# Squares of the queries in the second attention: two heads, two parts, one pass

## The chip, the cores and the metric

The kernel runs on one core of a Trainium2 chip. The metric is device time in microseconds (us), the median of several runs. The inputs are fixed, all in 32-bit floats; everything from the first layer norm to the last output is one program.

## The reference, cut to what matters

The program computes two layers on 625 nodes with 768 features: graph convolutions, attention with random features, and feed-forward parts, the last of them a mixture of experts. The change lies in the attention of the second layer:

```python
def _phi(t, random_features):                  # t: 12 heads, 625 nodes, 64
    norm_sq = 0.5 * jnp.sum(t * t, axis=-1, keepdims=True)
    proj = jnp.einsum('bhnd,md->bhnm', t, random_features)      # 256 features
    return jnp.exp(proj - norm_sq) * (1.0 / math.sqrt(M))
q_p = _phi(q, random_features)
k_p = _phi(k, random_features)
kv = jnp.einsum('bhnm,bhnd->bhmd', k_p, v)
out = jnp.einsum('bhnm,bhmd->bhnd', q_p, kv)
normalizer = jnp.einsum('bhnm,bhm->bhn', q_p, jnp.sum(k_p, axis=2))[..., None]
out = out / (normalizer + 1e-06)
```

For each query and head, minus half of the sum of its 64 squares is added to each of its 256 projections, ahead of the exponential.

## The kernel before, in words

`phase_attend` (L259) is called twice, the second time with `second=True`; only that call is touched. It treats the 12 heads as 6 pairs. A pair's queries lie with the feature on the partitions: head 0 in rows 0 to 63, head 1 in rows 64 to 127 (`own(hd)`; `other(hd)` is the other 64 rows), and 628 columns of nodes, in two halves of 314.

A 32-bit product is made of parts. A value is split into a high part, rounded by a copy into the type F32R (ScalarE), and a low part, the rest (a subtraction on VectorE, or on GpSimd for the squares). `qk[:, QUERIES, hd]` holds one head's high part in its own 64 rows and its low part in the other 64, so that one pass over 128 rows adds both.

The squares are laid out in another way before the change: `sqf` (in `x_sb`) holds the full squares of both heads, `sq[:, a, 0, :]` their high part and `sq[:, a, 1, :]` their low part, each with both heads in its 128 rows (`a` is 1 for keys, 0 for queries). ScalarE writes `sqf` and the high part with two activations of 128x628 (`squares`, L607 and L608) and GpSimd the low part (`square_low`, L354).

TensorE makes the query features in `features_q` (L434): for each of four tiles `m` of 128 features (two for head 0, two for head 1), four matmuls against the random features (L454), then four with `nh` as the weights (L462): parts `a` = 0, 1 times column halves `h` = 0, 1. `nh` is 128x512 with -0.5 in one head's rows and 0 in the other's, so that it picks the head. `key_norms` (L400) uses two of its columns (L409).

The order of the work is written out by hand, each engine with a queue of its own, tied by semaphores. For pair `p`:

- TensorE: `key_norms`, five tiles of key features (L428), with the projections of pair `p+1` between them (L191); four tiles of query features with projections between them; keys times values (L514, 40 matmuls); three more projections; `attend` (L191, out of `m_phiq`, `m_kv`). `attend` waits for `kv_lo`, which VectorE signals at L859.
- ScalarE: five key tiles, each two exponentials (L647) and a copy (L651); the high parts of the keys of `p+1` (L595); for each query tile an exponential (L669) and one that writes the high part (L670), with the key squares of `p+1` after tile 0; a weight chunk's high part (L128); the parts of kv (L684, L688); the query high parts of `p+1`; the denominators (L711); and `squares(p+1, QUERIES)`, which stands right ahead of the key tiles of `p+1`.
- VectorE: the low parts of the five key tiles (L815), with two quarters of a reciprocal (L773) after tiles 0 and 2; key low parts (L764); query low parts (L835) with two more reciprocals and a product (L777) ahead of tile 2; the weight chunk's low part (L139); kv (L853 to L859); copies (L885).
- GpSimd: the low parts of the squares, keys and queries in turn.

ScalarE's exponential of key tile `t` (from tile 2 on) waits for the low part of tile `t-2` (`pk_lo`), which frees its buffer `pf`. TensorE's query tile `m` (from 2 on) waits for the high part of tile `m-2` (`pq_hi`).

Ahead of the pairs, the last five value tiles (`values(2)`, L365) run on TensorE, with the squares of pair 0, a chunk's split (L128, L139) and the value splits (L583, L740) on the other engines; a value tile waits for the low part of the last but one.

Of the kernel before, what the change touches and what calls it, by code (L numbers as in the profile page):

```python
# [6 lines left out]
F32 = mybir.dt.float32  # L7
F32R = mybir.dt.float32r
# [9 lines left out]
P = 128  # L18
# [177 lines left out]
def halves(t):  # L196

    return t.rearrange("p (h n) -> p h n", h=2)
# [60 lines left out]
def phase_attend(k, name, second, rf=None):  # L259
# [3 lines left out]
    with ExitStack() as ctx:  # L263
# [17 lines left out]
        if second:  # L281
            scratch = k.x[:].rearrange("p t d -> p (t d)")
            pf = scratch[:, 0:2 * NT].rearrange("p (a n) -> p a n", a=2)
            sqf = scratch[:, 2 * NT:4 * NT].rearrange("p (a n) -> p a n", a=2)
            den = scratch[:, 4 * NT:5 * NT]
            sq = k.sb(f"{name}_sq", [P, 2, 2, NT], F32R)
            nh = k.sb(f"{name}_nh", [P, 512], F32R)
            key_norm = k.sb(f"{name}_key_norm", [P, 2 * TT], F32)
            tiny = k.sb(f"{name}_tiny", [P, 1], F32)
            k.x_dram = k.nc.dram_tensor("x_dram", (NODES, D), F32).ap()  # L290
        else:
            bv, bq, bp = k.v_bias, k.qk_bias, k.out_bias
        s = signals(k, name, (
            "saved", "rf_in", "chain", "ones_set", "rf_turned", "rf_bd", "rf_hi", "rf_ready", "kn_mm", "kn_f", "v_mm", "v_f", "v_hi",
            "v_lo", "qk_mm", "qk_hi", "qk_lo", "sq_hi", "sq_lo", "pk_mm", "pk_f", "pk_hi", "pk_lo",
            "pq_mm", "pq_f", "pq_hi", "pq_lo", "by_mm", "by_act", "by_dve", "kv_mm", "kv_part", "kv_f", "kv_hi", "kv_lo", "at_mm", "den_f", "num_f",
            "at_out"))
        st.freed.update({n: (s["v_mm"], TT * (c + 1)) for c, n in enumerate(V_CHUNK)})
# [7 lines left out]
        def qk_count(p, a):  # L306
            return 2 * p + (1 if a == KEYS else 2)
# [34 lines left out]
        @block.gpsimd  # L342
        def _(pool):
            k.clear_last(pool)

            def square_low(p):
                for a in (KEYS, QUERIES):
                    pool.wait_ge(s["sq_hi"], qk_count(p, a))
                    if p >= 1:
                        if a == KEYS:  # L350
                            pool.wait_ge(s["pk_mm"], TT * p)
                        else:
                            pool.wait_ge(s["pq_mm"], 4 * p)
                    pool.tensor_tensor(sq[:, a, 1, :], sqf[:, a, :], sq[:, a, 0, :].bitcast(F32), ALU.subtract)\  # L354
                        .then_inc(s["sq_lo"], 1)

            if second:
                for p in range(PAIRS):
                    square_low(p)

        @block.tensor
        def _(pe):
# [37 lines left out]
            def key_norms(p):  # L400
                pe.wait_ge(s["sq_lo"], qk_count(p, KEYS))
                if p >= 1:
                    pe.wait_ge(s["pk_f"], TT * p)
                    pe.wait_ge(s["pq_hi"], 4 * p)
                    pe.wait_ge(s["den_f"], 2 * p - 1)
                    pe.wait_ge(s["num_f"], 2 * p - 1)
                for t in range(TT):
                    for a in range(2):
                        mm = pe.matmul(norm_bank()[0:TS[t], 2 * t:2 * t + 2], sq[:, KEYS, a, t * P:t * P + TS[t]],  # L409
                                       nh[:, MF - 1:MF + 1], start=(a == 0), stop=(a == 1))  # L410
                mm.then_inc(s["kn_mm"], 1)

            def features_k(p):
# [20 lines left out]
            def features_q(p):  # L434
                for m in range(4):
                    i = p * 4 + m
                    if m == 0:
                        pe.wait_ge(s["qk_lo"], qk_count(p, QUERIES))
                        if p == 0:
                            pe.wait_ge(s["v_lo"], 3 * TT)  # L440
                        elif second:
                            pe.wait_ge(s["den_f"], 2 * p)
                            pe.wait_ge(s["num_f"], 2 * p)
                        else:
                            pe.wait_ge(s["num_f"], 2 * p)
                    if m == 1:
                        pe.wait_ge(s["pk_hi"] if second else s["pk_lo"], TT * (p + 1))
                    if m >= 2:
                        pe.wait_ge(s["pq_hi"] if second else s["pq_lo"], i - 1)
                    pair = query_pair(m)  # L450
                    hd, e = divmod(m, 2)
                    for a in range(2):
                        for h in range(2):
                            mm = pe.matmul(pair[:, h, 0:HN], rf2[:, a, e * P:(e + 1) * P],  # L454
                                           qk[:, QUERIES, hd, h * HN:(h + 1) * HN],
                                           start=(a == 0), stop=(a == 1 and not second))
                    if second:
                        if m == 0:
                            pe.wait_ge(s["sq_lo"], qk_count(p, QUERIES))
                        for a in range(2):  # L460
                            for h in range(2):
                                mm = pe.matmul(pair[:, h, 0:HN], nh[:, m * P:(m + 1) * P],  # L462
                                               sq[:, QUERIES, a, h * HN:(h + 1) * HN], start=False, stop=(a == 1))
                    mm.then_inc(s["pq_mm"], 1)
                    if second and p == PAIRS - 1 and m == 1:
                        lead_unit(0)
                    if second and m < 3:
                        project_unit(p + 1, KD + m)
                    elif m == 1:
                        for u in range(KD, KD + 3):  # L470
                            project_unit(p + 1, u)
# [98 lines left out]
        def _(act):  # L570
# [29 lines left out]
            def squares(p, a):  # L600
                src = qk_pair[a][:, :, 0:HN]
                if p == 0:
                    act.wait_ge(s["saved"], 16 * len(ROWS))
                else:
                    act.wait_ge(s["sq_lo"], qk_count(p - 1, a))
                act.wait_ge(s["qk_lo"], qk_count(p, a))
                act.activation(halves(sqf[:, a, :]), src, ACT.Square)  # L607
                act.activation(halves(sq[:, a, 0, :]), src, ACT.Square).then_inc(s["sq_hi"], 1)  # L608

            if not second:  # L610
                ring_high(act, st, 1)
# [110 lines left out]
        def _(dve):  # L722
            link = Link(dve, s["chain"])
            if second:
                dve.memset(vt[:, :, :, DH + 1:DH + 2].bitcast(F32), 0.0)
                dve.memset(kvf[:], 0.0)
                dve.memset(tiny[:], 1e-6)
                dve.memset(nh[:].bitcast(F32), 0.0)
                link(dve.memset(vt[:, :, :, DH:DH + 1].bitcast(F32), 1.0))
                for hd in range(2):  # L730
                    ins = dve.memset(nh[own(hd), hd * MF:(hd + 1) * MF].bitcast(F32), -0.5)
                link(ins)

            def v_low(i):
# [3514 lines left out]
```

## Time and profile before

| what | us |
|---|---|
| median of 3 runs | 1971.12 |
| lowest and highest run | 1968.50, 1972.91 |
| span of the profiled execution, first to last instruction | 1967.0 |
| TensorE busy in it | 1883.6 (96%) |
| VectorE busy | 1205.9 (61%) |
| ScalarE busy | 872.9 (44%) |
| GpSimd busy | 93.9 (5%) |

Of the profiled execution the profile gives the span alone; the runs' median is 4.1 us above it. The second attention's pairs lie between about 992 and 1157 us of the span. In the rows, PE is TensorE, PEld its weight loads, ACT is ScalarE, DVE is VectorE, POOL is GpSimd; a row's text in brackets is the idle time of the engine before it and what ended it.

### The profile page before, as it was taken

The page shows a single profiled execution, that of the slowest core. Times are in us where ns is not written, and L with a number is a line of the kernel's source. Part 1 is how long each engine was busy: PE and PEld are TensorE (multiplying, and loading weights), DVE is VectorE, ACT ScalarE, POOL GpSimd, SP SyncE. Part 2 cuts the span into 40 slices and gives each one's busy share as a digit, 9 for nine tenths or more (in the row PEclk, how much of TensorE's full clock was granted, in tenths as well). Part 3 has the DMA queues.
Part 4 walks back from the last instruction along what each step waited for, and adds up shares of the span by engine and source line. Part 5 has one row for each costly group of instructions (what it writes and reads, how often), then busy time and mean ns, then how long its engine had stood idle before and what let it go on. Part 6 is the DMA issues. An engine that isn't in the chain of part 4 may idle for free. (4 is left out here: it accounts for less than half of the span.)

```text
span 1967.0 us, 32303 instructions
## 1 busy us (share of the span) xinstructions
PE 1883.6 (96%) x13051; PEld 1776.8 (90%) x13051; DVE 1205.9 (61%) x1909; ACT 872.9 (44%) x1176; POOL 93.9 (5%) x84
## 2 busy tenths in 40 slices
PE   5899899999999999998999989899999999999999
PEld 4899789999999999998899989798878888888899
DVE  8467786444343345445557777675666668889732
ACT  6456622222111212214377762423655557777620
POOL 0000000000000000000011000100111101100000
PEclk7899999999999999999999999899999999999999
DMA  3311235121111112110211041424877679999831
GB/s 92 98 41 41 61 105 124 57 57 57 58 57 57 52 45 85 49 49 17 90 33 33 17 142 52 160 77 165 296 234 245 211 231 332 369 379 375 296 119 40
DMA packets 157962, 250.53 MB, mean 127 GB/s; under 512 B 11949, under 2 KB 86189, under 8 KB 157460
## 3 DMA queue, kind: packets, MB, share of 16 engines
q1 hardware_dynamic: 152532, 231.21, 35.3%
q0 software_dynamic: 5040, 17.56, 3.7%
q8 instruction: 89, 1.46, 0.3%
q14 instruction: 29, 0.24, 0.0%
q10 hardware_dynamic: 272, 0.07, 0.0%
HBM read 228.80 MB, written 20.01 MB: 126 GB/s over the span
## 5 line engine op out<-in xcount | busy, mean ns | idle before, releaser
L183 PE MATMUL psum<-products_room 128*128 128x512 f32 (+2 forms) x2160 | 457.2, 366 | 3.1 <-DVE re_credit L3728 2.0
L183 PEld LDWEIGHTS psum<-products_room 128*128 128x128 f32 (+1 forms) x2160 | 388.5, 187 | 47.1 <-issue 2.3
L183 PE MATMUL psum<-ring_hi,xt_sb 128*128 128x256 f32 (+3 forms) x1920 | 357.0, 284 | 9.7 <-PEq L1285 2.8
L3625 DVE TENSOR_TENSOR products_room<-moe_raw,products_room 128x1536 fp32r<-128x1536 f32 x179 | 312.4, 1754 | 76.8 <-ACT products_room L3524 76.4
L3524 ACT ACTIVATE products_room<-moe_raw 128x1536 fp32r<-128x1536 f32 x179 | 266.0, 1489 | 151.9 <-PE psum L183 83.6
L183 PEld LDWEIGHTS psum<-ring_hi,xt_sb 128*128 128x128 f32 (+1 forms) x1920 | 301.2, 189 | 11.5 <-issue 6.3
L183 PE MATMUL psum<-ring_lo,xt_sb 128*128 128x256 f32 (+3 forms) x960 | 271.4, 283 | 0.0
L183 PEld LDWEIGHTS psum<-ring_lo,xt_sb 128*128 128x128 f32 (+1 forms) x960 | 181.5, 189 | 0.0
L183 PE MATMUL psum<-ring_hi,gnn_sb 128*128 128x256 f32 (+1 forms) x810 | 150.0, 286 | 5.4 <-DVE gnn_sb L1188 3.6
L139 DVE TENSOR_TENSOR ring_lo<-ring_raw,ring_hi 128x1536 fp32r<-128x1536 f32 (+1 forms) x64 | 119.4, 1865 | 50.6 <-ACT ring_hi L128 50.5
L191 PE MATMUL psum<-xt_sb,ring_hi 128*128 128x314 f32 x744 | 140.0, 310 | 0.3
L128 ACT ACTIVATE ring_hi<-ring_raw 128x1536 fp32r<-128x1536 f32 (+1 forms) x65 | 101.9, 1568 | 81.5 <-PE psum L191 32.2
L183 PEld LDWEIGHTS psum<-ring_hi,gnn_sb 128*128 128x128 f32 (+1 forms) x810 | 127.2, 191 | 6.3 <-issue 4.3
L191 PE MATMUL psum<-xt_sb,products_room 128*128 128x314 f32 x864 | 127.3, 309 | 2.1 <-DVE products_room L4068 1.1
L191 PEld LDWEIGHTS psum<-xt_sb,products_room 128*128 128x128 f32 x864 | 126.0, 189 | 2.8 <-issue 1.4
L1702 ACT ACTIVATE g_y<-psum 128x256 fp32r<-128x256 f32 (+3 forms) x100 | 37.7, 378 | 198.6 <-PE psum L1635 104.0
L1751 DVE TENSOR_TENSOR g_y<-psum,g_y 128x256 fp32r<-128x256 f32 (+3 forms) x100 | 41.5, 417 | 134.2 <-ACT g_y L1702 134.0
L1656 PE MATMUL psum<-gnn_sb,g_y 128*128 128x314 f32 (+1 forms) x780 | 117.2, 308 | 0.0
L183 PE MATMUL psum<-ring_lo,gnn_sb 128*128 128x256 f32 (+1 forms) x405 | 115.7, 286 | 0.0
L191 PEld LDWEIGHTS psum<-xt_sb,ring_hi 128*128 128x128 f32 x744 | 114.5, 189 | 1.0 <-issue 1.0
L1656 PEld LDWEIGHTS psum<-gnn_sb,g_y 128*128 128x128 f32 (+1 forms) x780 | 114.3, 190 | 0.3 <-DVE g_cnt L1727 0.3
L191 PE MATMUL psum<-xt_sb,ring_lo 128*128 128x314 f32 x372 | 84.7, 309 | 0.0
(532 smaller groups left out, 2756.8 us busy)
## 6 DMA issues: line engine op xcount, KB each, us to landing
moe_raw<-in_L_ffn_Wg_r SPq DMA_DIRECT2D x60, 768.0 KB, 6.1
moe_raw<-in_L_ffn_Wu_r SPq DMA_DIRECT2D x60, 768.0 KB, 6.0
moe_raw<-in_L_ffn_Wd_r SPq DMA_DIRECT2D x60, 768.0 KB, 8.7
ring_raw<-in_L_gnn_w_rel SPq DMA_DIRECT2D x18, 896.0 KB, 5.1
ring_raw<-in_L_mix_W_qkv SPq DMA_DIRECT2D x24, 384.0 KB, 4.3
ring_raw<-in_L_gnn_w_rel SPq DMA_DIRECT2D x9, 768.0 KB, 4.5
ring_raw<-in_L_gnn_w_root SPq DMA_DIRECT2D x6, 896.0 KB, 5.1
count_total_dram<-gnn_sb POOLq DMA_DIRECT2D x3, 1570.0 KB, 11.2
```

What stands on the lines that cost most here:

```text
L128: act.activation(ring.hi[:, g % RING_SLOTS, 0:size], ring.raw[:, g % RING_SLOTS, 0:size], ACT.Copy).then_inc(ring.hi_done, 1)
L139: dve.tensor_tensor(lo, raw, hi.bitcast(F32), ALU.subtract).then_inc(ring.lo_done, 1)
L183: mm = pe.matmul(out, lhs[a], rhs[b], start=(first and i == 0), stop=(last and i == 2))
L191: mm = pe.matmul(bank_pair[:, h, 0:HN], lhs[a], rhs(b, h), start=(first and i == 0), stop=(last and i == 2))
L1656: mm = pe.matmul(pair[:, h, 0:HN], y[0:TS[t], v % 2, t, a, col + m * P:col + (m + 1) * P], k.C[0:TS[t], r, t, h * HN:(h + 1) * HN], start= ...
L1702: act.activation(y[0:TS[t], v % 2, t, 0, 0:w], k.banks[i % 3][0:TS[t], 0:w], ACT.Copy).then_inc(s["y_hi"], 1)
L1751: dve.tensor_tensor(y[0:TS[t], v % 2, t, 1, 0:w], k.banks[i % 3][0:TS[t], 0:w], y[0:TS[t], v % 2, t, 0, 0:w].bitcast(F32), ALU.subtract).t ...
L3524: act.activation(whi[:, slot, :], raw[i % RAWS], ACT.Copy).then_inc(s["hi_done"], 1)
L3625: dve.tensor_tensor(wlo[:, i % RING, :], raw[i % RAWS], whi[:, i % RING, :].bitcast(F32), ALU.subtract)\
```

## The change

The query squares are kept by head. `sq[:, QUERIES, hd]` now holds head `hd`'s high part in its own 64 rows and its low part in the other 64, as `qk` does. With a 128x128 tile of -0.5 (`minus_half`) as weights, one pass adds both. The keys stay as they were.

```diff
-            nh = k.sb(f"{name}_nh", [P, 512], F32R)
+            nh = k.sb(f"{name}_nh", [P, 2], F32R)
+            minus_half = k.sb(f"{name}_minus_half", [P, P], F32R)
...
             def square_low(p):
-                for a in (KEYS, QUERIES):
-                    pool.wait_ge(s["sq_hi"], qk_count(p, a))
-                    if p >= 1:
-                        if a == KEYS:
-                            pool.wait_ge(s["pk_mm"], TT * p)
-                        else:
-                            pool.wait_ge(s["pq_mm"], 4 * p)
-                    pool.tensor_tensor(sq[:, a, 1, :], sqf[:, a, :], sq[:, a, 0, :].bitcast(F32), ALU.subtract)\
-                        .then_inc(s["sq_lo"], 1)
+                pool.wait_ge(s["sq_hi"], qk_count(p, KEYS))
+                if p >= 1:
+                    pool.wait_ge(s["pk_mm"], TT * p)
+                pool.tensor_tensor(sq[:, KEYS, 1, :], sqf[:, KEYS, :], sq[:, KEYS, 0, :].bitcast(F32), ALU.subtract)\
+                    .then_inc(s["sq_lo"], 1)
+                pool.wait_ge(s["sq_hi"], qk_count(p, QUERIES))
+                if p >= 1:
+                    pool.wait_ge(s["pq_mm"], 4 * p)
+                pool.wait_ge(s["sq_lo"], qk_count(p, KEYS))
+                for hd in range(2):
+                    if hd == 1:
+                        pool.wait_ge(s["sq_half"], p + 1)
+                    ins = pool.tensor_tensor(sq[other(hd), QUERIES, hd, :], sqf[own(hd), QUERIES, :],
+                                             sq[own(hd), QUERIES, hd, :].bitcast(F32), ALU.subtract)
+                    ins.then_inc(s["sq_half"] if hd == 0 else s["sq_lo"], 1)
+                if p + 1 < PAIRS:
+                    pool.wait_ge(s["sq_lo"], qk_count(p, QUERIES))
...
-                                       nh[:, MF - 1:MF + 1], start=(a == 0), stop=(a == 1))
+                                       nh[:], start=(a == 0), stop=(a == 1))
...
-                        for a in range(2):
-                            for h in range(2):
-                                mm = pe.matmul(pair[:, h, 0:HN], nh[:, m * P:(m + 1) * P],
-                                               sq[:, QUERIES, a, h * HN:(h + 1) * HN], start=False, stop=(a == 1))
+                        for h in range(2):
+                            mm = pe.matmul(pair[:, h, 0:HN], minus_half[:], sq[:, QUERIES, hd, h * HN:(h + 1) * HN],
+                                           start=False, stop=True)
...
                 act.activation(halves(sqf[:, a, :]), src, ACT.Square)
-                act.activation(halves(sq[:, a, 0, :]), src, ACT.Square).then_inc(s["sq_hi"], 1)
+                if a == KEYS:
+                    act.activation(halves(sq[:, a, 0, :]), src, ACT.Square).then_inc(s["sq_hi"], 1)
+                    return
+                for hd in range(2):
+                    ins = act.activation(halves(sq[own(hd), a, hd, :]), qk_pair[a][own(hd), :, 0:HN], ACT.Square)
+                ins.then_inc(s["sq_hi"], 1)
...
                 dve.memset(nh[:].bitcast(F32), 0.0)
                 link(dve.memset(vt[:, :, :, DH:DH + 1].bitcast(F32), 1.0))
+                dve.memset(minus_half[:].bitcast(F32), -0.5)
                 for hd in range(2):
-                    ins = dve.memset(nh[own(hd), hd * MF:(hd + 1) * MF].bitcast(F32), -0.5)
+                    ins = dve.memset(nh[own(hd), hd:hd + 1].bitcast(F32), -0.5)
                 link(ins)
```

## Rows read from the trace of the kernel before

**Rows 1.** Windows, the stretch of one pair: busy us (instructions), clock, DMA.

```profile
1048.10:1075.50 27.40, 26.86 (x201) 26.59 (x200) 19.79 (x28) 20.93 (x38) 3.08 (x2) 1.00 0.10 30
```

**Rows 2.** Timeline of ScalarE, one pair: start us, us, engine, line, operation.

```profile
1048.08 0.69 ACT L607 ACTIVATE x_sb<-psum 128x628 f32<-128x628 f32 x1
1048.67 0.69 ACT L608 ACTIVATE m_sq<-psum 128x628 fp32r<-128x628 f32 x1
1049.38 0.84 ACT L647 ACTIVATE x_sb<-psum,m_key_norm 128x256 f32<-128x256 f32 x2
...
1050.79 0.82 ACT L647 ACTIVATE x_sb<-psum,m_key_norm 128x256 f32<-128x256 f32 x2
...
1056.35 1.39 ACT L595 ACTIVATE m_qk<-psum 64x628 fp32r<-64x628 f32 x2
...
1060.67 0.72 ACT L670 ACTIVATE m_phiq<-psum 128x628 fp32r<-128x628 f32 x1
...
1063.28 0.69 ACT L669 ACTIVATE x_sb<-psum 128x628 f32<-128x628 f32 x1 [0.71 <-PE psum L462]
```

**Rows 3.** Timeline of VectorE, the same pair.

```profile
1050.92 0.69 DVE L815 TENSOR_TENSOR m_phik<-x_sb,m_phik 128x512 fp32r<-128x512 f32 x1 [2.43 <-ACT m_phik L651]
...
1052.57 0.63 DVE L815 TENSOR_TENSOR m_phik<-x_sb,m_phik 128x512 fp32r<-128x512 f32 x1
...
1059.08 0.81 DVE L835 TENSOR_TENSOR m_phiq<-x_sb,m_phiq 128x628 fp32r<-128x628 f32 x1 [0.24 <-ACT m_phiq L670]
1061.42 1.08 DVE L835 TENSOR_TENSOR m_phiq<-x_sb,m_phiq 128x628 fp32r<-128x628 f32 x1 [1.53 <-ACT m_phiq L670]
...
1066.76 1.75 DVE L139 TENSOR_TENSOR ring_lo<-ring_raw,ring_hi 128x1536 fp32r<-128x1536 f32 x1
1068.54 0.29 DVE L853 SCALAR_TENSOR_TENSOR m_kvf<-psum,m_kvt 128x128 f32<-128x128 f32 x1
```

**Rows 4.** Timeline of TensorE, the end of the same pair.

```profile
1062.50 0.74 PE L462 MATMUL psum<-m_sq,m_nh 128*128 128x314 f32 x4
1063.08 4.58 PE L514 MATMUL psum<-m_v,m_phik 128*128 128x130 f32 x40
...
1070.86 3.33 PE L191 MATMUL psum<-m_phiq,m_kv 128*128 128x314 f32 x21 [0.54 <-DVE m_kv L859]
```

**Rows 5.** Timeline of GpSimd, the same pair: query squares, then key squares.

```profile
1049.43 1.55 POOL L354 TENSOR_TENSOR m_sq<-x_sb,m_sq 128x628 fp32r<-128x628 f32 x1 [14.99 <-ACT m_sq L608]
1060.29 1.54 POOL L354 TENSOR_TENSOR m_sq<-x_sb,m_sq 128x628 fp32r<-128x628 f32 x1 [9.31 <-ACT m_sq L608]
```

**Rows 6.** Timeline after the attention: GpSimd and VectorE at the same time.

```profile
1234.13 1.87 POOL L2557 TENSOR_TENSOR x_sb<-x_sb,p_y 113x768 f32<-113x768 f32 x1
...
1234.73 1.28 DVE L1825 TENSOR_TENSOR tmp<-rstd 128x3 f32<-128x3 f32 x1
...
1241.85 0.16 DVE L1825 TENSOR_TENSOR tmp<-rstd 128x2 f32<-128x2 f32 x1
```

**Rows 7.** Timeline of GpSimd and VectorE during the last value tiles.

```profile
984.93 3.06 POOL L354 TENSOR_TENSOR m_sq<-x_sb,m_sq 128x628 fp32r<-128x628 f32 x2 [48.31 <-ACT m_sq L608]
...
988.17 1.76 DVE L139 TENSOR_TENSOR ring_lo<-ring_raw,ring_hi 128x1536 fp32r<-128x1536 f32 x1 [0.95 <-ACT ring_hi L128]
...
989.85 0.42 DVE L740 TENSOR_TENSOR m_v<-psum,m_v 128x256 fp32r<-128x256 f32 x1
```

**Rows 8.** Timeline of VectorE and TensorE at the start of the phase.

```profile
958.30 0.48 DVE L728 MEMSET m_nh<- 128x512 f32 x1
...
959.01 0.64 DVE L731 MEMSET m_nh<- 64x256 f32 x2
...
960.59 0.35 PE L183 MATMUL psum<-ring_hi,xt_sb 128*128 128x256 f32 x1 [0.58 <-DVE m_v L740]
```

**Rows 9.** Timeline, the first pair (ScalarE) and the last (TensorE).

```profile
1008.87 0.70 ACT L669 ACTIVATE x_sb<-psum 128x628 f32<-128x628 f32 x1 [0.35 <-PE psum L462]
...
1138.64 0.85 PE L454 MATMUL psum<-m_qk,m_rf 128*128 128x314 f32 x4 [1.54 <-ACT m_phik L651]
```

More of the change, by code:

```diff
@@ L294, in phase_attend @@
             "saved", "rf_in", "chain", "ones_set", "rf_turned", "rf_bd", "rf_hi", "rf_ready", "kn_mm", "kn_f", "v_mm", "v_f", "v_hi",
-            "v_lo", "qk_mm", "qk_hi", "qk_lo", "sq_hi", "sq_lo", "pk_mm", "pk_f", "pk_hi", "pk_lo",
+            "v_lo", "qk_mm", "qk_hi", "qk_lo", "sq_hi", "sq_half", "sq_lo", "pk_mm", "pk_f", "pk_hi", "pk_lo",
             "pq_mm", "pq_f", "pq_hi", "pq_lo", "by_mm", "by_act", "by_dve", "kv_mm", "kv_part", "kv_f", "kv_hi", "kv_lo", "at_mm", "den_f", "num_f",
```

## The prediction

> **What bounds the kernel now.** The page first: TensorE is busy 96% of the span, so a change that takes matmuls away looks like a gain. That share is a mean, so I read the windows of the pairs next: a middle pair takes 27.40 us, of which TensorE is busy 26.86 and ScalarE 20.93 [rows 1]. TensorE idles 0.54 us a pair, and the timeline says where: `attend` waits for VectorE's L859 [rows 4]. Someone else ends last there, by little. Following that wait back gives the loop of the pair:
>
> - VectorE runs without a gap from its L835 of query tile 1 at 1061.42 to the end of L139 at 1068.51, and L853, which feeds L859, starts 0.03 us later [rows 3]. ScalarE's L684, its other input, ended at 1068.14 in the timeline, so VectorE's own queue ends 0.4 us after TensorE's side.
> - That L835 waited 1.53 us for ScalarE's L670 of tile 1, which ended at 1061.39 [rows 2, 3].
> - ScalarE has no idle time from the query squares at 1048.08 to there: squares, five key tiles (1.39 us each), L595, tiles 0 and 1. Its first wait on TensorE is at tile 3 [rows 2]. The squares follow L711, which waits for `attend` of the pair before.
>
> So in pairs 1 to 4 the loop is attend, ScalarE, VectorE, attend. TensorE's matmuls in `features_q` stand beside it, and the query squares stand in it.
>
> **Part by part.** *Matmuls.* Four norm matmuls take 0.58 us of TensorE (1062.50 to 1063.08), an issue every 0.145 us [rows 4]; two of four go in each of 24 tiles: 24 x 0.29 = 7.0 us of TensorE work. In pairs 1 to 4 I count this as nothing: tile 3 starts when ScalarE has finished tile 1 (1061.39; it started 0.58 ahead of the row at 1062.50, at 1061.92), and TensorE would arrive 0.9 us sooner only to wait.
>
> *ScalarE.* Two activations become three: the full squares and two of 64x628. L607 to L608 start 0.59 us apart, while the pair of L595, also 64x628, takes 1.39 us, 0.70 each, without overlap [rows 2]. More work per pair is thus 0.59 to 0.81 us (one more step at the short pace; or two at 0.70 for one at 0.59). I take 0.70. It lies in the loop, behind L711 and ahead of the key tiles.
>
> The Trainium skill (ScalarE: Activation LUTs, section "What ACT_TABLE_LOAD costs") says that back-to-back activations overlap by about 93 ns. Here 128-row ones do (0.69 long, 0.59 apart), two of 64 rows in different halves don't; by the rule each pair would cost 0.1 us less.
>
> *GpSimd.* One 128x628 subtraction of 1.55 us [rows 5] becomes two of 64x628 that read one half and write the other. No row shows either. Bounds: 0.8 us each if the time goes by rows, 3.1 each if crossing costs a second pass. I take 1.55, since VectorE's and ScalarE's rows of 64 partitions last as long as those of 128. GpSimd is then busy 3.1 us instead of 1.55. The results are needed by tile 0's norm matmuls, which stand behind the last key tile (its L595 starts at 1056.35), with 3 us to spare, so TensorE doesn't wait for them. The other waits added on GpSimd hold nobody else: nothing but these squares stands in its queue.
>
> *What GpSimd does to VectorE.* A VectorE TENSOR_TENSOR of 128x3 took 1.28 us, to 1236.01, while GpSimd's L2557 ran to 1236.00; the same line takes 0.16 alone [rows 6]. And L835 of tile 1, beside the key squares that ended at 1061.83, took 1.08 instead of 0.81 [rows 3, 5]. A two-input VectorE operation from SBUF stands still until GpSimd's is done. Two places meet the longer GpSimd work:
>
> - Key tiles, pairs 1 to 5. Call E the end of ScalarE's squares (1049.36, later 1050.06). GpSimd's first half runs from E+0.07 to E+1.62. L815 of tile 0 comes at E+1.56 as before, where it suffers nothing today (0.69 us) [rows 3]. The second half must first see the first's semaphore, so I let L815 go first; it runs to E+2.2, and the second half from there to E+3.8. L815 of tile 1, due at E+3.2, then ends near E+4.4 instead of E+3.8. ScalarE's key tile 3 is due at E+4.2 and waits for it: 0.25 us, in the loop.
> - The value tiles ahead of pair 0. The squares end 0.7 us later, near 987.0; GpSimd's halves run to 988.6 and 990.2. L128, behind the squares on ScalarE, brings L139 to 988.87 instead of 988.17 [rows 7]; it stands until 990.2 and ends at 991.85 instead of 989.93. Behind it in VectorE's queue is L740 of value tile 12, and TensorE's value tile 14 waits for that; it started at 990.4, right after it [rows 7]. Cost 1.9 us, on the path; 0.7 if GpSimd were out of the way.
>
> The Trainium skill (SBUF — State Buffer, section "Who interferes with whom") states this as a rule: a tensor_tensor with both inputs in SBUF and a GpSimd instruction that reads SBUF exclude each other, and whoever comes first keeps the port for its whole instruction. These rows agree.
>
> *Memsets.* `nh` shrinks from 512 columns (0.48 us) and two halves of 256 (0.64) to 2 columns, and 128 columns are added: about 1.12 becomes 0.35 (0.06 for a tiny one, and a quarter of 0.42 more for 128). VectorE starts its value splits 0.77 us sooner, and TensorE's wait of 0.58 for them goes [rows 8]. Next it is bound by itself. Gain 0.6.
>
> *Pair 0.* It has no reciprocals, and TensorE leads: ScalarE waited 0.35 for tile 3 [rows 9]. Tile 3 still starts after ScalarE's tile 1, so only its own 0.29 is won. *Pair 5.* No work for a next pair stands on ScalarE; TensorE waits for key tile 4 (1.54) [rows 9]. That comes 0.95 later, and three tiles behind it save 0.87: 0.1 lost.
>
> **Sum:** -0.6 (memsets) + 1.9 (value tiles) - 0.3 (pair 0) + 4 x 0.95 (pairs 1 to 4) + 0.1 (pair 5) = +4.9 us. The profiled span goes from 1967.0 to 1971.9. The median of the runs lies 4.1 above that span; I keep this and get 1976.0. What follows the attention waits for it and passes the shift on, since its loads need the memory that the attention holds.
>
> **The rivals.** *The loop takes ScalarE's 0.7 but GpSimd is in nobody's way* (halves of 0.8 us, or L139 gets in between them): -0.6 + 0.7 - 0.3 + 4 x 0.7 - 0.2 = +2.4, 1973.5. For it: half the rows are half the data. Against: the rows of 64 partitions on other engines.
>
> *GpSimd's second half goes ahead of L815*: L815 of tile 0 then ends at E+3.8, key tile 2 waits 1.1 us for it and tile 3 another 0.25. Pairs 1 to 4 cost 2.05 each and pair 5 1.2: -0.6 + 1.9 - 0.3 + 8.2 + 1.2 = +10.4, 1981.5. For it: L815 and the gap between the halves lie within 0.1 us. With halves of 3.1 us both would block, some 4 us a pair, near 1990.
>
> *ScalarE's work is absorbed* (the loop has slack that I don't see): only memsets, pair 0 and pair 5 remain, about -1, 1970.
>
> *Faster: TensorE paces the pairs.* If TensorE's side ended last at `attend`, the 7.0 us would come off, with the memsets' 0.6: 1963.5. For it are 26.86 busy of 27.40. It decides where VectorE's queue is done before ScalarE's L684; today it is 0.4 us behind, and the change puts 0.95 more on that side and takes 1.2 from TensorE's.
>
> **How the numbers follow.** Forecast 0.45; GpSimd out of the way 0.2; GpSimd first or slow 0.2; absorbed 0.1; faster 0.05. The time is 1976.0. The range runs from the absorbed case to a little past the third: 1970.5 to 1982.5, leaving out the fast case and the far end of slow halves. What can be told from no change is 0.2%, 3.9 us; the forecast's 4.9 is just past it, and with runs spread by 4 us it may fall on either side. Slower: two thirds of the first case, a quarter of the second, nearly all of the third, 0.55. Faster 0.06, same 0.39.
>
> **What would show it.** In the profile of the changed kernel: L462's successor 48 times and not 96; three squares of queries taking about 2.0 us from the first to the key tiles, not 1.30; the pair's length 28.3, not 27.4; TensorE's wait at `attend` about 1.3 us and new waits ahead of tiles 2 and 3; GpSimd's halves at 1.5 us; L139 near 988.9 lasting 3 us; the 0.58 us wait at 960.6 gone. Pairs of 27.4 or less would make the prediction wrong at its root; GpSimd's halves far from 1.5 us, or L815 of tile 0 at 2 us, would move it to a rival.

## The result

| | median, us | lowest and highest | runs |
|---|---|---|---|
| before | 1969.66 | 1966.42, 1972.91 | 8 |
| after | 1975.27 | 1972.88, 1977.93 | 8 |

The ratio is 1.0029, with a 95% interval of 1.0021 to 1.0038: 5.6 us slower (4.1 to 7.5), where +4.9 was forecast. The profiled execution of after has a span of 1975.1 us, 8.1 more than that of before.

The first line of its page:

```profile
span 1975.1 us, 32221 instructions
```

Next the window of the pair that [rows 1] shows of before, with the same columns:

```profile
1050.30:1078.60 28.30, 26.55 (x193) 25.46 (x193) 20.24 (x29) 21.63 (x40) 5.02 (x3) 1.00 0.09 29
```

TensorE is idle for 1.75 us of it (28.30 less 26.55) where it was idle for 0.54, and ScalarE is busy 0.70 us more. ScalarE, against [rows 2]:

```profile
1050.35 0.70 ACT L615 ACTIVATE x_sb<-psum 128x628 f32<-128x628 f32 x1
1050.94 1.38 ACT L620 ACTIVATE m_sq<-psum 64x628 fp32r<-64x628 f32 x2
1052.34 0.84 ACT L660 ACTIVATE x_sb<-psum,m_key_norm 128x256 f32<-128x256 f32 x2
...
1055.15 0.82 ACT L660 ACTIVATE x_sb<-psum,m_key_norm 128x256 f32<-128x256 f32 x2
...
1056.62 0.84 ACT L660 ACTIVATE x_sb<-psum,m_key_norm 128x256 f32<-128x256 f32 x2
```

The key tiles start 1.99 us after the squares, not 1.30. Tile 3 (1056.62) starts 1.47 us after tile 2 (1055.15), not 1.39 as the tiles of before: a wait of 0.08, where I had taken 0.25. These two, and 0.04 in which a query tile's low part stands longer behind GpSimd's key squares (1.12 us, 1.08 before), make 0.81 of the 0.85 that the pair grows by in the ledger below. The reason for the wait of 0.08 lies on VectorE and GpSimd, against [rows 3, 5]. First VectorE, then GpSimd:

```profile
1053.88 0.69 DVE L829 TENSOR_TENSOR m_phik<-x_sb,m_phik 128x512 fp32r<-128x512 f32 x1 [3.12 <-ACT m_phik L664]
...
1055.54 1.82 DVE L829 TENSOR_TENSOR m_phik<-x_sb,m_phik 128x512 fp32r<-128x512 f32 x2
...
1069.87 1.75 DVE L139 TENSOR_TENSOR ring_lo<-ring_raw,ring_hi 128x1536 fp32r<-128x1536 f32 x1
...
1071.65 0.29 DVE L867 SCALAR_TENSOR_TENSOR m_kvf<-psum,m_kvt 128x128 f32<-128x128 f32 x1
```

```profile
1052.40 3.57 POOL L360 TENSOR_TENSOR m_sq<-x_sb,m_sq 64x628 fp32r<-64x628 f32 x2 [15.68 <-ACT m_sq L620]
```

L829 is the low part of a key tile, L815 before the change. That of tile 0 went first, with its usual 0.69 us, and GpSimd's second half ran until 1055.97; the next two L829 took 1.82 us together instead of some 1.3. The last two rows of VectorE are the ones that decide: L139 and then, 0.03 us behind it, L867, as L853 stood behind L139 in [rows 3]. Now TensorE, from the query tiles to `attend`, against [rows 4]:

```profile
1062.16 0.85 PE L463 MATMUL psum<-m_qk,m_rf 128*128 128x314 f32 x4 [0.16 <-ACT m_phiq L683]
...
1064.51 0.85 PE L463 MATMUL psum<-m_qk,m_rf 128*128 128x314 f32 x4 [0.34 <-ACT m_phiq L683]
1065.19 0.46 PE L470 MATMUL psum<-m_sq,m_minus_half 128*128 128x314 f32 x2
1065.49 4.58 PE L522 MATMUL psum<-m_v,m_phik 128*128 128x130 f32 x40
...
1073.98 2.31 PE L191 MATMUL psum<-m_phiq,m_kv 128*128 128x314 f32 x14 [1.25 <-DVE m_kv L873]
```

From their start to the next line the two norm matmuls (L470) take 0.30 us where four took 0.58, and what they save turns into idle time: new waits of 0.16 and 0.34 us ahead of query tiles 2 and 3, and 1.25 us at `attend` instead of 0.54. The three make the 1.75 of the window.

The ledger of the phase comes from three starts that each trace has: TensorE's first matmul of the phase, ScalarE's second denominators (L711 of before) of each pair, and TensorE's first matmul behind the phase. All times are of one profiled execution each; the last row of the table also has 1.27 us between the last denominators and that matmul, the same in both.

| us | before | after | difference | predicted |
|---|---|---|---|---|
| start of the phase | 957.66 | 958.24 | +0.6 | 0 |
| to the end of pair 0 | 62.22 | 63.07 | +0.85 | +1.0 |
| pairs 1 to 4, each | 27.37 to 27.39 | 28.22 to 28.25 | +0.85 | +0.95 |
| pair 5 | 26.16 | 28.70 | +2.54 | +0.1 |
| whole phase | 199.19 | 205.97 | +6.78 | +4.9 |

The span grew by 8.1 us: 0.6 ahead of the phase, 6.8 in it and 0.7 behind it. A second profiled execution of the changed kernel gave 28.21 to 28.24 for pairs 1 to 4, 27.56 for pair 5 and 204.82 for the phase. So pairs 1 to 4 are steady and pair 5 isn't. The windows of pair 5 (the same columns, the clock third from the end), first before, then after:

```profile
1130.20:1156.80 26.60, 20.88 (x154) 19.54 (x153) 14.74 (x25) 15.85 (x31) 1.53 (x1) 1.00 0.01 2
```

```profile
1135.00:1164.20 29.20, 23.59 (x146) 22.12 (x147) 15.32 (x25) 16.68 (x33) 3.48 (x2) 0.82 0.00 1
...
1141.70:1149.80 8.10, 7.34 (x31) 6.95 (x31) 5.72 (x8) 4.89 (x10) 0.00 (x0) 0.50 0.01 2
```

TensorE's granted clock is at half speed, the 1.2 GHz level, for at least 8.1 us in the middle of the pair. TensorE's timeline shows what it did before, against [rows 9]:

```profile
1137.93 0.74 PE L437 MATMUL psum<-m_rf,m_qk 128*128 128x256 f32 x4 [1.62 <-ACT x_sb L660]
...
1140.71 1.19 PE L437 MATMUL psum<-m_rf,m_qk 128*113 128x256 f32 x4 [0.64 <-ACT x_sb L660]
1141.71 1.25 PE L463 MATMUL psum<-m_qk,m_rf 128*128 128x314 f32 x4
1142.75 0.73 PE L470 MATMUL psum<-m_sq,m_minus_half 128*128 128x314 f32 x2
...
1144.23 1.41 PE L463 MATMUL psum<-m_qk,m_rf 128*128 128x314 f32 x4 [0.76 <-ACT m_phik L664]
...
1150.58 0.45 PE L470 MATMUL psum<-m_sq,m_minus_half 128*128 128x314 f32 x2
```

Four matmuls of L463 take 1.25 us here and 0.75 to 0.85 elsewhere; L470 takes 0.73 and later 0.45 again. In this pair no projections of a next pair stand between the key tiles. TensorE waits for ScalarE ahead of tiles 2, 3 and 4, and since ScalarE starts 0.7 us later the first of these waits is longer than in before, where the row is

```profile
1132.42 0.74 PE L428 MATMUL psum<-m_rf,m_qk 128*128 128x256 f32 x4 [0.94 <-ACT x_sb L647]
```

The value tiles and the start of the phase, against [rows 7] and [rows 8]: GpSimd, VectorE and TensorE at the value tiles, then VectorE's memsets.

```profile
986.87 3.17 POOL L360 TENSOR_TENSOR m_sq<-x_sb,m_sq 64x628 fp32r<-64x628 f32 x2 [0.58 <-ACT m_sq L620]
...
988.61 3.04 DVE L139 TENSOR_TENSOR ring_lo<-ring_raw,ring_hi 128x1536 fp32r<-128x1536 f32 x1 [0.95 <-ACT ring_hi L128]
...
992.04 0.38 PE L183 MATMUL psum<-ring_hi,xt_sb 128*113 128x256 f32 x1 [1.68 <-DVE m_v L754]
```

```profile
958.78 0.06 DVE L741 MEMSET m_nh<- 128x2 f32 x1
959.05 0.17 DVE L743 MEMSET m_minus_half<- 128x128 f32 x1
959.16 0.16 DVE L745 MEMSET m_nh<- 64x1 f32 x2
```

L139 started at 988.61, stood while GpSimd's second half ran to 990.04, and took 3.04 us instead of 1.76. The value tile behind it waited 1.68 us; before, it didn't wait.

### The profile page after: what moved, and what is told of

Same layout as the page of the kernel before. It is cut to its first block and busy times, and to the rows that moved or that the text cites. A ratio compares the mean times of both kernels' runs of the same rounds, so it can differ in the third digit from the quotient of the medians.

```text
span 1975.1 us, 32221 instructions
## 1 busy us (share of the span) xinstructions
PE 1884.7 (95%) x13003; PEld 1773.2 (90%) x13003; DVE 1209.0 (61%) x1910; ACT 877.4 (44%) x1182; POOL 105.3 (5%) x90
## 5 line engine op out<-in xcount | busy, mean ns | idle before, releaser
L139 DVE TENSOR_TENSOR ring_lo<-ring_raw,ring_hi 128x1536 fp32r<-128x1536 f32 (+1 forms) x64 | 120.7, 1886 | 51.3 <-ACT ring_hi L128 51.2
L128 ACT ACTIVATE ring_hi<-ring_raw 128x1536 fp32r<-128x1536 f32 (+1 forms) x65 | 101.9, 1568 | 81.0 <-PE psum L191 32.2
```

Of the source, the lines that this page charges most:

```text
L128: act.activation(ring.hi[:, g % RING_SLOTS, 0:size], ring.raw[:, g % RING_SLOTS, 0:size], ACT.Copy).then_inc(ring.hi_done, 1)
L139: dve.tensor_tensor(lo, raw, hi.bitcast(F32), ALU.subtract).then_inc(ring.lo_done, 1)
```

## Experiments

Each median stands beside that of before, measured alongside it on the same chip; the chips of the three groups of experiments differ. "Phase" is the ledger's length; 199.19 is before's.

**Each half of the change alone.** First GpSimd's halves in the kernel before:

```diff
+                    for hd in range(2):
+                        if hd == 1:
+                            pool.wait_ge(s["sq_half"], p + 1)
+                        ins = pool.tensor_tensor(sq[own(hd), a, 1, :], sqf[own(hd), a, :],
+                                                 sq[own(hd), a, 0, :].bitcast(F32), ALU.subtract)
```

> The kernel before, with one edit: GpSimd makes the low part of the query squares in two operations of 64 rows, the second behind the first's semaphore, instead of one of 128. ScalarE and TensorE do what they did. Theory (GpSimd's second half stands in VectorE's way): GpSimd busy 3.1 to 3.6 us a pair for the queries; L139 ahead of pair 0, at 988.2, is held until about 989.6 and ends 1.3 us later, and TensorE's last value tile with it; in pairs 1 to 4 the low part of key tile 1 ends about 1 us late and ScalarE's key tile 3 loses about 0.1 us. Sum +1.3 + 0.4 + 0.1 = +1.8 us on 1969.7. Rival (GpSimd is in nobody's way): 0.

Measured: 1970.86 against 1969.49, ratio 1.0008 [0.9999, 1.0017]; phase 201.10, +1.9. Pairs 1 to 4 took 27.50 to 27.52 (+0.12), the part to the end of pair 0 63.54 (+1.32). VectorE and TensorE at the value tiles:

```profile
987.68 3.06 DVE L139 TENSOR_TENSOR ring_lo<-ring_raw,ring_hi 128x1536 fp32r<-128x1536 f32 x1 [0.95 <-ACT ring_hi L128]
...
991.13 0.38 PE L183 MATMUL psum<-ring_hi,xt_sb 128*113 128x256 f32 x1 [1.06 <-DVE m_v L748]
```

GpSimd's halves alone make L139 3.06 us long. Here each half stays in its own rows, so the crossing to the other half is not what costs. Pair 5 took 26.25 us, 0.09 more than before, at a granted clock of 0.93.

Then ScalarE's:

```diff
-                act.activation(halves(sq[:, a, 0, :]), src, ACT.Square).then_inc(s["sq_hi"], 1)
+                for hd in range(2):
+                    ins = act.activation(halves(sq[own(hd), a, 0, :]), qk_pair[a][own(hd), :, 0:HN], ACT.Square)
+                ins.then_inc(s["sq_hi"], 1)
```

> The kernel before, with one edit: ScalarE writes the high part of the query squares in two activations of 64 rows instead of one of 128, in the old layout. GpSimd and TensorE do what they did. Theory (ScalarE stands in the loop): 0.70 us a pair from the squares to the key tiles, pairs 1 to 4 28.1 us instead of 27.4, L139 ahead of pair 0 0.7 us later but not held, pair 5 +0.7: +0.7 + 4 x 0.7 + 0.7 = +4.2 us; if TensorE's clock also falls in pair 5, as it did in the changed kernel's profile, about 2 us more. Rival (ScalarE's work is absorbed, GpSimd makes all of the loss): 0 to 1 us.

Measured: 1974.54 against 1969.49, ratio 1.0022 [1.0013, 1.0031]; phase 203.50, +4.3. Pairs 1 to 4 took 28.08 to 28.13, +0.71: ScalarE's 0.70 us comes through whole. L139 keeps its length:

```profile
989.14 1.76 DVE L139 TENSOR_TENSOR ring_lo<-ring_raw,ring_hi 128x1536 fp32r<-128x1536 f32 x1 [0.96 <-ACT ring_hi L128]
```

Pair 5 took 26.94 us, 0.78 more than before. TensorE's work in it is that of before, and yet its clock fell: the first wait at the key tiles, and the window of the pair, are

```profile
1136.97 1.22 PE L428 MATMUL psum<-m_rf,m_qk 128*128 128x256 f32 x4 [1.63 <-ACT x_sb L652]
```

```profile
1134.10:1161.50 27.40, 23.29 (x155) 21.68 (x154) 14.78 (x24) 16.58 (x32) 1.52 (x1) 0.88 0.00 1
```

The two halves add up for the pairs: 0.71 and 0.12 make 0.83 of the 0.85.

**Are the matmuls worth anything?** The changed kernel, with its norm passes made twice at half the weight:

```diff
-                dve.memset(minus_half[:].bitcast(F32), -0.5)
+                dve.memset(minus_half[:].bitcast(F32), -0.25)
...
+                        for a in range(2):
                             for h in range(2):
-                                           start=False, stop=True)
+                                               start=False, stop=(a == 1))
```

> The changed kernel, with the two norm matmuls of each query tile made four again: each pass is added twice with weights of -0.25. Theory (in pairs 1 to 4 TensorE waits for ScalarE and VectorE anyway): pairs 1 to 4 stay at 28.25 us; pair 0 loses 0.3; pair 5 loses 0.9 where the clock falls as before. Against the changed kernel +1.2 us, or about -1 if the busier TensorE keeps its clock in pair 5. Rival (TensorE paces the pairs): 24 x 0.29 = +7.0 us.

Measured: 1975.17 against 1969.49, ratio 1.0027 [1.0016, 1.0038], where after's is 1.0029. Pairs 1 to 4 took 28.23 to 28.28, as in after. To the end of pair 0 it lost 0.31. So the 48 matmuls that the change took away are worth nothing where ScalarE and VectorE pace, and 0.3 us in pair 0, as forecast. Pair 5 took 26.96 us, with more matmuls in it, at a granted clock of 0.88: 1.7 and 0.6 less than in the two profiles of after, and as long as with ScalarE's halves alone.

**The value tiles.** The changed kernel, with the weight chunk's low part two value splits later:

```diff
-                v_low(2 * TT)
-                v_low(2 * TT + 1)
-                ring_low(dve, st, 4)
-                for i in range(2 * TT + 2, 3 * TT):
+                for i in range(2 * TT, 2 * TT + 4):
                     v_low(i)
+                ring_low(dve, st, 4)
+                v_low(2 * TT + 4)
```

> The changed kernel, with one edit on VectorE's queue ahead of pair 0: the weight chunk's low part (L139) stands behind the low parts of value tiles 12 and 13, not ahead of them. Theory (L139, held by GpSimd's query halves, held value tile 12's split and TensorE's last value tile by 1.7 us): TensorE's wait of 1.68 us goes, L139 runs near 991.6 to 993.4, just ahead of its first use near 994, and the time falls by 1.7 us against the changed kernel, to about 1973.6. Rival (the wait is made up later, since ScalarE paces pair 0): 0.

Measured: 1973.26 against 1969.49, ratio 1.0017 [1.0008, 1.0026]; to the end of pair 0 61.12, 1.95 less than after. VectorE:

```profile
990.81 1.75 DVE L139 TENSOR_TENSOR ring_lo<-ring_raw,ring_hi 128x1536 fp32r<-128x1536 f32 x1
```

L139 starts when GpSimd is done and takes its own 1.75 us, and TensorE no longer waits. That fits the term of 1.9. With L139 out of the way pair 0 ends 1.10 us sooner than in before, where the forecast gave the memsets and pair 0's matmuls 0.9 together.

**Pair 5 and the clock.** The changed kernel, with six matmuls after each key tile of pair 5 (30 in all, into a PSUM tile that nobody reads):

```diff
                     project_unit(p + 1, t)
+                    if second and p == PAIRS - 1:
+                        fill()
```

> The changed kernel, with six matmuls more behind each of pair 5's five key tiles, where the other pairs have a projection. They write a bank that is free there and nobody reads, so the result is the same; 30 matmuls of work are added. Theory (pair 5 cost 28.7 us instead of 26.2 because TensorE, idle behind ScalarE's key tiles, lost its clock, and ran the rest at half speed): the clock stays at 1.00 in pair 5 and the pair takes about 26.2 us, 2.4 less than in the changed kernel, though TensorE does more. Rival (the loss in pair 5 is a wait for ScalarE or GpSimd, and the clock only a mark of it): 28.4 or more, time as the changed kernel's or a little above.

Measured: pair 5 took 26.09 instead of 28.70, the phase 203.32. The window of pair 5:

```profile
1135.10:1161.70 26.60, 23.57 (x176) 22.58 (x176) 15.16 (x25) 16.68 (x33) 3.49 (x2) 1.00 0.01 2
```

With more work the clock stays at full speed, and the pair is as short as before's. But the runs' median is 1974.74 against 1970.07, ratio 1.0027 [1.0015, 1.0039], not told apart from after's. The second profile of the changed kernel was to say how steady the loss is:

> The changed kernel again, for one more profile. Theory: pairs 1 to 4 28.2 us each, TensorE's wait of 1.7 us ahead of the last value tile, and the clock at half for some us in pair 5, with the pair above 28 us. Rival (the clock in pair 5 is an accident of one execution): pair 5 near 26.3 us at full clock.

Measured: one run, 1976.12, and in its profile

```profile
1135.30:1163.30 28.00, 23.31 (x146) 21.68 (x146) 15.27 (x24) 16.63 (x32) 3.47 (x2) 0.82 0.00 1
```

the same clock and 27.56 us. The loss is there in both profiles of after, at 1.4 and 2.5 us. The profiles of all the experiments, those below included, say more. "Norm matmuls" are those of pair 5's query tiles; the two columns behind them are the first wait ahead of a key tile and the mean clock over the pair:

| pair 5 in | norm matmuls | wait, us | clock | us |
|---|---|---|---|---|
| before, and before with the split moved (last experiment) | 16 | 0.94 | 1.00 | 26.16, 26.18 |
| GpSimd's halves alone | 16 | 0.93 | 0.93 | 26.25 |
| ScalarE's halves alone | 16 | 1.63 | 0.87 | 26.94 |
| after with doubled passes | 16 | 1.63 | 0.87 | 26.96 |
| after (two profiles), with the split later, with the split moved | 8 | 1.62 | 0.81 to 0.82 | 28.70, 27.56, 28.37, 27.48 |
| after, filled | 8, and 30 more | none | 1.00 | 26.09 |
| squares on VectorE, and filled | 8 | 0.39, none | 1.00 | 24.91, 24.89 |
| squares on VectorE, split moved | 8 | 0.39 | 0.93 | 26.25 |

The clock fell in all six profiles with the wait of 1.6 us, whether or not matmuls had been taken away. ScalarE's longer squares are enough for that; with the eight matmuls gone as well it was lower still, and the pair 0.5 to 1.8 us longer. Fewer matmuls without the longer wait (the squares on VectorE) left the clock at 1.00. Two rows (0.93) show a fall without that wait, and no run says what brings it there.

**A version without the cost.** ScalarE writes only the full squares of the queries; VectorE makes the high and low parts, by head as in the change; GpSimd has the keys alone. The split goes later as above, and the reciprocals move behind the next key tile. The same kernel with the 30 added matmuls in pair 5 was run too.

```diff
+            def query_high(p):
+                dve.wait_ge(s["sq_full"], p + 1)
+                for hd in range(2):
+                    ins = dve.tensor_copy(sq[own(hd), QUERIES, hd, :], sqf[own(hd), QUERIES, :])
+                ins.then_inc(s["sq_hi"], 1)
+
+            def query_low(p, hd):
+                if hd == 0:
+                    dve.wait_ge(s["sq_hi"], qk_count(p, QUERIES))
+                ins = dve.tensor_tensor(sq[other(hd), QUERIES, hd, :], sqf[own(hd), QUERIES, :],
+                                        sq[own(hd), QUERIES, hd, :].bitcast(F32), ALU.subtract)
...
+                    if second and t in (0, 2):
+                        query_low(p, t // 2)
```

> The changed kernel's layout and its two norm matmuls, with the query squares made in another place: ScalarE writes the full squares alone (one activation), VectorE copies the high parts ahead of key tile 0 and subtracts the low parts behind key tiles 0 and 2 (its reciprocals move behind tiles 1 and 3), GpSimd has the keys only, and L139 ahead of pair 0 stands behind value tiles 12 and 13. Theory (ScalarE's query squares are in the loop, VectorE has room ahead of tile 0 and GpSimd's work collides): pairs 1 to 4 take 26.8 us, 0.6 less than before the change and 1.45 less than after it; pair 0 ends 0.9 sooner than before the change; pair 5 24.7, or some 2 us more if the clock falls. Time against the kernel before: -4.8 us, or -2.8 with the fall of the clock. Rival (VectorE becomes the bound: four operations of 0.8 us a pair on it): pairs of 28 us and more, slower than before.

> The kernel on_vector (the query squares split on VectorE) with the 30 added matmuls of the kernel filled in pair 5. Theory: if the clock falls in pair 5 of on_vector, it stays here, and the time is some 2 us below on_vector; against the kernel before -4.8 us. If the clock doesn't fall in on_vector, the two are equal within 0.5 us. Rival (added matmuls delay TensorE, which has nothing to spare once ScalarE is shorter): 0.5 to 1 us above on_vector.

Measured: 1966.70 and 1969.22 against 1970.07, ratios 0.9988 [0.9979, 0.9997] and 1.0003 [0.9994, 1.0012]. Pairs 1 to 4 took 27.54 and 27.56, not the 26.8 expected; pair 5 24.91 and 24.89, both at full clock, so the fill had nothing to mend there. Three timelines of the first: VectorE, ScalarE, TensorE.

```profile
1045.84 0.98 DVE L774 CAST m_sq<-x_sb 64x628 fp32r<-64x628 f32 x2 [0.32 <-ACT x_sb L603]
...
1048.13 0.81 DVE L780 TENSOR_TENSOR m_sq<-x_sb,m_sq 64x628 fp32r<-64x628 f32 x1
```

```profile
1056.15 0.70 ACT L603 ACTIVATE x_sb<-psum 128x628 f32<-128x628 f32 x1 [0.36 <-DVE m_qk L764]
```

```profile
1068.07 3.74 PE L191 MATMUL psum<-m_phiq,m_kv 128*128 128x314 f32 x24 [1.20 <-DVE m_kv L877]
```

ScalarE now waits for VectorE (L764), and TensorE waits 1.20 us at `attend`: with 2 x 0.49 and 2 x 0.81 us more in its queue, VectorE took ScalarE's place in the loop. The phase is 198.31 and 198.32, 0.9 below before in both: 1.25 less in pair 5 and 0.25 to 0.3 up to the end of pair 0, against 0.6 to 0.7 more in pairs 1 to 4. Their medians differ by 2.5 us all the same. In the profiles the difference stands ahead of the phase (it starts at 954.80 and 957.89, behind the same code), so 0.9 us of the ratio's 2.4 is shown to come from the edit, and the rest isn't.

**Does VectorE's queue set the end of a pair?** In three kernels (before, after, and the one above) the weight chunk's split was moved: its high part behind the query high parts of the next pair, its low part (L139) to the next pair's first query tile, out of the way of L853. GpSimd's key squares wait until the query tiles' low parts are done, so as not to meet L139.

```diff
+                    pool.wait_ge(s["pq_lo"], 4 * p)
...
-                if second and p + 5 <= len(st.chunks):
+                if second and p == 0:
-                    ring_low(dve, st, p + 5)
+                    ring_low(dve, st, 5)
...
+                    if m == 0 and second and 1 <= p and p + 5 <= len(st.chunks):
+                        ring_low(dve, st, p + 5)
```

> The kernel before, with two steps moved for pairs 1 to 4. The weight chunk's split leaves the end of VectorE's queue: ScalarE makes the high part (L128) at the end of the pair before, behind the query high parts, and VectorE the low part (L139) behind query tile 0, where it is idle for 1.5 us. GpSimd's key squares wait until VectorE's query tiles are done, so as not to meet L139. Squares and norm matmuls are as before the change. Theory (VectorE's queue ends 0.4 us after TensorE's side at attend, so taking 1.75 us off it wins only that): pairs 1 to 4 27.05 us instead of 27.4, time -1.4 us against the kernel before. Rival (the chunk's split was the bound by its whole length): -1.75 x 4 = -7 us.

> The changed kernel with the same two moves. Theory (after the change VectorE's queue ends 1.2 us after TensorE's side; with it shortened, attend follows query tile 3, which waits for ScalarE's tile 1, 0.3 us later than before the change and with 0.3 us less of matmuls behind it): pairs 1 to 4 27.1 us instead of 28.2, time -4.5 us against the changed kernel, near 1970.8, as the kernel before within 0.2%. Rival (ScalarE's longer squares come through whatever VectorE does): pairs near 27.9, -1.5 us.

> The kernel on_vector (query squares split on VectorE) with the same two moves. In on_vector TensorE waited 1.2 us at attend for VectorE's queue, pairs 27.54 us. Theory (VectorE's queue had become the bound): the kv chain then starts behind ScalarE's copy, 1.0 us sooner, pairs 1 to 4 26.55 us, time -4 us against on_vector, near 1963 and the fastest of all. Rival (L139 behind tile 0 delays VectorE's tile 1 and gives it back): pairs near 27.4, no change.

Measured, against 1970.84:

| kernel with the split moved | median | ratio | pairs 1 to 4 | phase |
|---|---|---|---|---|
| before | 1969.60 | 0.9998 [0.9989, 1.0007] | 27.02 to 27.34 | 199.22 |
| after | 1970.83 | 1.0006 [0.9998, 1.0015] | 27.14 to 27.16 | 201.00 |
| parts on VectorE | 1967.96 | 0.9988 [0.9977, 0.9998] | 26.53 to 26.89 | 197.13 |

The changed kernel gets 1.1 us a pair back in pairs 1 to 4, 4.3 in all, loses 0.58 up to the end of pair 0, and stands within 0.1% of before, as expected. (The phase is 4.97 shorter than in the first profile of after and 3.82 than in the second: the difference is pair 5.) Its `attend`, and VectorE's row ahead of it:

```profile
1097.19 0.29 DVE L872 SCALAR_TENSOR_TENSOR m_kvf<-psum,m_kvt 128x128 f32<-128x128 f32 x1 [0.89 <-ACT m_kvt L698]
```

```profile
1099.51 3.74 PE L191 MATMUL psum<-m_phiq,m_kv 128*128 128x314 f32 x24 [0.19 <-DVE m_kv L878]
```

VectorE idles 0.89 us before it and TensorE waits 0.19 instead of 1.25: VectorE's queue was what ended last. The move takes L128 out of ScalarE's queue as well, but that was in nobody's way: in after ScalarE stood idle for 1.74 us between L128 and the parts of kv. In before the same move gave 0.37 us in pair 1 and 0.05 to 0.09 in each of the next three, where 0.35 each was expected, and nothing over the phase (199.22 against 199.19), as it lost 0.57 up to the end of pair 0. With the parts on VectorE pairs 1 to 4 became shorter by 0.65 to 1.01 us each, 3.06 in all, which shows VectorE's queue as their bound. But the part to the end of pair 0 grew by 0.54 and pair 5 by 1.34, at the lower clock of the table, so the phase is 1.18 shorter, and the time near 1963 that was expected didn't come: the ratio to before is 0.9988 with and without the moved split.

## Why the prediction was right

Its likeliest case came: +5.6 us where +4.9 was forecast, 1975.27 against 1976.0. Point by point:

- *What bounds the pair.* The loop through ScalarE and VectorE was shown from both sides: doubling the norm matmuls leaves a pair at 28.23 to 28.28, and taking L139 from the end of VectorE's queue brings it from 28.2 to 27.15.
- *ScalarE, 0.70 a pair.* Measured 0.69 from the squares to the key tiles, and 0.71 in the pair when made alone. The estimate came from the pair of L595 of the same shape, and not from the pace of 128 rows. The Trainium skill's 93 ns of overlap (ScalarE: Activation LUTs, section "What ACT_TABLE_LOAD costs") is seen here between activations of 128 rows (0.70 us long, 0.59 apart) and not between two of 64 rows in different halves (1.38 for two).
- *GpSimd, 1.55 each.* 3.17 us for two at the value tiles: right. That L829 of tile 0 goes first was right as well; but the wait of key tile 3 was mis-sized, 0.08 instead of 0.25. With GpSimd's halves alone the pairs grew by 0.12. The queue of VectorE has idle time between the key tiles that took in the rest.
- *Value tiles, +1.9.* L139 took 3.04 us, and going out of GpSimd's way gave 1.95 back. In time it was close too (988.61, forecast 988.9). The Trainium skill's exclusive lock between a two-input VectorE operation and GpSimd (SBUF — State Buffer, section "Who interferes with whom") agrees with these rows: L139 started 0.15 us after GpSimd's second half, when that had 1.43 us to run, and took 1.28 us longer than alone.
- *Memsets, -0.6 and pair 0, -0.3.* The 0.58 us wait is gone; with the value tiles the ledger has +0.85 for +1.0. The 0.3 was shown by the doubled passes (0.31). The memsets were not changed by themselves; their -0.6 rests on the wait that went.
- *Pair 5, +0.1.* This is the step that was wrong: +2.5 and +1.4 in two profiles. The sum took the full clock for granted. TensorE idled longer ahead of a key tile (1.62 us, not 0.94), and its granted clock then fell to the 1.2 GHz level. That the lost time is the clock's is shown by the filled version, 26.09 us with the same ScalarE and GpSimd work and 30 matmuls more: at full clock the term of +0.1 came as -0.07. The prediction set the three shorter tiles against ScalarE's 0.95, but ScalarE's work alone lowered the clock (0.87), and the profiles with the shorter tiles are the ones with the lowest clock (0.81 to 0.82).
- *The level.* This was wrong, and luck that it did so little. I carried over that the runs' median lies 4.1 us above the profiled span, which compared different executions. Where both figures of one execution are known, a run of before lies 1.7 to 1.8 us above its own span and a run of after 2.0 to 2.1. The 1971.12 that the 1976.0 was built on was a median of three runs; that of eight is 1969.66, 1.5 lower. The change came out 0.7 larger than forecast, the two went against each other, and 1976.0 missed 1975.27 by only 0.7.

The rivals fell on single rows: GpSimd out of the way (L139 would have stayed at 1.76), GpSimd first (L829 of tile 0 would have been 2 us long), absorbed and faster (pairs would have been 27.4 or less).

Open: what pair 5's clock costs in the runs that weren't profiled. All four profiles with the change's queues in pair 5 lost 1.3 to 2.5 us there, so the loss is common; but the runs' difference doesn't size it. The phase is 6.8 us longer in the first profile of after, 5.6 in the second and would be 4.2 without pair 5's loss, for 5.6 [4.1, 7.5] measured.

## What to carry to other kernels

An engine that is busy 96% of the time need not pace a loop: look at which wait ends last in one round, and at what stands right ahead of it in the other engine's queue. Two half-height operations cost about twice a full one on all three other engines here (128x628 against 64x628: a VectorE subtraction 0.81 and 0.81 us each, a ScalarE square 0.69 and 0.69, a GpSimd subtraction 1.55 and 1.55), so a layout that saves matmuls by splitting work by partitions is paid for elsewhere. Where TensorE already waits for another engine, a change that makes it wait longer can lower its clock (here 0.7 us of ScalarE work was enough), and matmuls taken away in the same stretch then save nothing.

## What I had not expected of the hardware

- TensorE's granted clock fell to 0.50 for at least 8.1 us in pair 5 of after, behind an idle time of 1.62 us and one of 0.65; with 30 matmuls more it stayed at 1.00. In before, with idle times of 0.94 and 0.65, it stayed at 1.00 too. With ScalarE's longer squares alone, and no matmul less than in before, the mean over the pair was 0.87.
- GpSimd's two halves took 3.17 us together at the value tiles, where they ran one behind the other, and 3.57 in the pairs, where VectorE's L829 (0.69 us) came in between.
- A VectorE copy of 64x628 from 32-bit into F32R takes 0.49 us, the subtraction of the same size 0.81.
- The stretch ahead of the phase, with the same code, ended between 954.25 and 958.86 us in the thirteen profiled executions, a spread nearly as large as what the change costs: the ledger of the phase tells such small changes apart better than the span does.
